# The first stage's instructions in another order, from a planner with other durations and priorities

## The reference, cut to what matters

```python
q, k, v = layernormed 4-to-1 channel mixes of layernorm(x)      # "read", three outputs of 256
o = causal softmax attention, 16 heads of 16, rope on q and k
h = h * A_full(o) + out(o) * B_full(o)                           # "write": softplus, exp, reciprocal
g, u = layernormed channel mixes of h
m = silu(g @ ctx...) * (u @ ctx...)                              # MLP to 1024
h = h * A_full(m) + out(m) * B_full(m)                           # second "write"
x = x + ...
W = mean_w + mean(|w - mean_w|) * sign(w - mean_w)               # for w1, w3, w2, 3584 x 1024 each
y = x + (silu(n @ W1.T) * (n @ W3.T)) @ W2.T                     # n = layernorm(x)
```

## Time and profile before

| | us |
|---|---|
| median of 3 runs | 1407.24 |
| lowest, highest | 1401.03, 1408.16 |
| the profiled execution, its own time | 1408.62 |
| its span in the trace | 1406.8 |
| mean granted TensorE clock over the span | 0.958 |

### The profile page before, as it was taken

One profiled execution on the slowest core, in us unless ns is written; L12 is line 12 of the kernel. 1 busy time (PEld: TensorE's weight loads), 2 busy tenths in 40 slices (PEclk: granted clock), 3 DMA queues, 4 the chain that ended last, 5 costly groups with the idle time before them and its releaser, 6 DMA issues.

```text
span 1406.8 us, 16747 instructions
## 1 busy us (share of the span) xinstructions
PE 1292.9 (92%) x6548; PEld 1015.8 (72%) x6548; DVE 868.6 (62%) x1135; ACT 530.1 (38%) x809; POOL 361.9 (26%) x197
## 2 busy tenths in 40 slices
PE   4887788877887899999999999999999999999998
PEld 4754555545665678888888888888788888888887
DVE  6768777778878865546564546363645546554544
ACT  4776665855655432222222222222222222222220
POOL 2222333233234422222222222222222222222210
PEclk9998988987899899999999999999999999999999
DMA  8476887577731222322222222232222232222312
GB/s 339 147 273 252 287 285 267 208 288 274 268 132 31 105 90 93 105 102 90 90 94 97 109 90 90 90 106 102 91 90 90 95 111 94 90 90 90 116 34 120
DMA packets 53826, 197.55 MB, mean 140 GB/s; under 512 B 6626, under 2 KB 6900, under 8 KB 53236
## 3 DMA queue, kind: packets, MB, share of 16 engines
q1 hardware_dynamic: 53748, 196.49, 38.7%
HBM read 192.27 MB, written 4.19 MB: 140 GB/s over the span
## 4 chain that ended last, share of the span: by engine, by line
PE 72%; DVE 15%; issue 5%; ACT 5%; DMA 2%; POOL 1%; SPq 0%; DVEq 0%; ACTq 0%
PE pair L969 42%; PE quad L1068 17%; PE pair L952 2%; DVE negwide L1372 2%; PE quad L915 1%; DMA ctxw<-in_mean_w 1%; DVE raw_w L1448 1%; DVE hid L1438 1%; PE pair L1022 1%; PE quad L905 1%; PE pair L843 1%; ACT prob L1122 1%; PE pair L824 1%; DVE wr_q L1425 1%; DVE big L1547 1%
## 5 line engine op out<-in xcount | busy, mean ns | idle before, releaser
L1633 POOL TENSOR_TENSOR raw_w<-raw_w,raw_base 128x1024 f32<-128x1024 f32 x84 | 215.5, 2567 | 661.5 <-DMA raw_base<-in_mean_w 661.5
L969 PE MATMUL pair<-xnT_hi,w_hi 128*128 128x512 f32 x880 | 343.8, 391 | 3.3 <-DVE xnT_lo L1557 3.3
L969 PE MATMUL pair<-xnT_lo,w_hi 128*128 128x512 f32 x880 | 343.6, 390 | 0.0
L969 PE MATMUL pair<-xnT_hi,w_lo 128*128 128x512 f32 x880 | 343.5, 390 | 0.0
L1590 DVE TENSOR_TENSOR hf<-sgf,pair 128x512 f32<-128x512 f32 x56 | 38.5, 688 | 282.1 <-PE pair L969 282.1
L1182 ACT ACTIVATE w_hi<-raw_w 128x1024 fp32r<-128x1024 f32 x84 | 88.8, 1058 | 324.0 <-DVE raw_w L1448 323.8
L969 PEld LDWEIGHTS pair<-xnT_hi,w_hi 128*128 128x128 f32 x880 | 166.1, 189 | 38.6 <-issue 2.7
L969 PEld LDWEIGHTS pair<-xnT_lo,w_hi 128*128 128x128 f32 x880 | 165.9, 189 | 34.5
L969 PEld LDWEIGHTS pair<-xnT_hi,w_lo 128*128 128x128 f32 x880 | 165.9, 189 | 34.4
L1068 PE MATMUL quad<-w_hi,h_hi 128*128 128x512 f32 x448 | 175.4, 391 | 9.3 <-DVE hid L1570 9.3
L1448 DVE SCALAR_TENSOR_TENSOR raw_w<-raw_w,coeff,raw_base 128x1024 f32<-128x1024 f32 x84 | 166.8, 1988 | 19.9 <-ACT raw_w L1165 19.9
(11 more groups left out here) (234 smaller groups left out, 1561.4 us busy)
## 6 DMA issues: line engine op xcount, KB each, us to landing
raw_w<-in_w SPq DMA_DIRECT2D x84, 512.0 KB, 3.8
raw_base<-in_mean_w SPq DMA_DIRECT2D x84, 512.0 KB, 4.6
part<-in_w SPq DMA_DIRECT2D x28, 512.0 KB, 4.1
part<-in_mean_w SPq DMA_DIRECT2D x28, 512.0 KB, 5.3
ctxw<-in_w SPq DMA_DIRECT2D x28, 512.0 KB, 4.8
ctxw<-in_mean_w SPq DMA_DIRECT2D x28, 512.0 KB, 6.3
big<-in_w SPq DMA_DIRECT2D x20, 512.0 KB, 3.8
big<-in_mean_w SPq DMA_DIRECT2D x20, 512.0 KB, 4.8
```

Of the source, the lines that this page charges most:

```text
L969: a = pe.matmul(banks[gate_bank(u, b)], ww[:, k, :], xx[:, k, :], start=k == 0 and n == 0, stop=k == KF - 1 and n == 2)
L1633: pool.tensor_tensor(w[:, :], w[:, :], base[:, :], ALU.subtract).then_inc(f_diff, 1)
```

## The change

Only the planner's inputs and its arithmetic are changed. The steps' durations on paper are set to other values; durations are multiplied by a factor per engine (`SLOW`, PE 1.107, DVE 1.061, ACT 1.009, POOL 0.981) in `engine_and_time` but not in `weight`; an engine is free for its next step a little before the step's result is done (`AHEAD_OF`, 0.04 to 0.16 us); a load takes the SP queue 0.8 us (`ISSUE`) and lands 1.6 us (`LANDING`) and its own duration later, but not before the load ahead of it has landed (`landed`); `HOP`, the time from one engine to another, is 0.05 in place of 0.12; and `FIRST`, `AHEAD`, `MEASURE_WEIGHT` and `PULL`, which set the priorities, all have other values. `OWN`, a lead for single steps, is empty. `LOADED`, `MEASURER`, `LATER`, the dependences and the program text of all engines are unchanged. What comes out is another order of the same steps on each engine, with the choices of banks that go with it.

```diff
@@ -112,38 +112,42 @@
 
 
 
-RAT = [("PE", 1.35), ("DVE", 0.3), ("PE", 0.25), ("ACT", 0.3), ("PE", 0.5), ("ACT", 1.7), ("DVE", 1.85, 0.2),
-       ("ACT", 0.87), ("DVE", 2.5, 0.25), ("POOL", 1.85), ("POOL", 0.75), ("DVE", 2.05, 2.05)]
+RAT = [("PE", 1.48), ("DVE", 0.27), ("PE", 0.27), ("ACT", 0.26), ("PE", 0.59), ("ACT", 1.48), ("DVE", 1.52, 0.2),
+       ("ACT", 0.83), ("DVE", 2.68, 0.25), ("POOL", 1.81), ("POOL", 0.72), ("DVE", 1.94, 1.94)]
 WORK = {
-    "front": [("DVE", 1.75), ("POOL", 0.6), ("DVE", 0.2, 0.15), ("ACT", 1.25), ("PE", 1.1), ("ACT", 1.05), ("PE", 1.95),
-              ("DVE", 1.95, 0.2), ("POOL", 0.9), ("DVE", 0.2, 0.15), ("ACT", 1.75), ("PE", 0.85), ("ACT", 2.8),
-              ("PE", 2.75), ("DVE", 2.95, 0.7), ("PE", 1.1), ("ACT", 1.22)],
-    "turnmax": [("PE", 0.35), ("DVE", 0.45)],
-    "out": [("ACT", 0.4)],
-    "row": [("PE", 0.6), ("DVE", 0.75), ("PE", 0.35), ("ACT", 0.4)],
-    "back": RAT + [("PE", 1.1), ("DVE", 1.25), ("PE", 1.95), ("DVE", 1.45, 0.2), ("POOL", 0.75), ("DVE", 0.2, 0.15),
-                   ("ACT", 1.15), ("PE", 0.6), ("ACT", 1.88)],
-    "mlp": [("PE", 1.85), ("ACT", 0.42), ("DVE", 0.45)],
-    "finish": [("PE", 5.25)] + RAT[1:8] + [("DVE", 3.5, 1.25)] + RAT[9:] + [("SP", 2.0), ("POOL", 0.75), ("DVE", 1.75), ("POOL", 0.6), ("DVE", 0.2, 0.15)],
-    "measure": [("SP", 3.5), ("POOL", 2.4), ("ACT", 1.17)],
-    "x": [("SP", 2.0)],
-    "ctx": [("SP", 7.0)],
-    "diag": [("DVE", 4.0, 4.0)],
-    "raw": [("SP", 2.0), ("POOL", 2.4), ("ACT", 1.06)],
-    "coef": [("DVE", 0.35), ("PE", 0.35), ("DVE", 0.2)],
-    "prep": [("DVE", 1.3, 1.3), ("ACT", 1.08), ("DVE", 1.25, 1.25)],
-    "norm": [("ACT", 1.25), ("PE", 1.1), ("ACT", 1.05), ("DVE", 1.25)],
-    "early": [("PE", 1.4)] * 4,
+    "front": [("DVE", 1.71), ("POOL", 0.55), ("DVE", 0.15, 0.15), ("ACT", 1.24), ("PE", 1.04), ("ACT", 1.02), ("PE", 1.92),
+              ("DVE", 1.64, 0.2), ("POOL", 0.86), ("DVE", 0.16, 0.16), ("ACT", 1.48), ("PE", 0.83), ("ACT", 2.19),
+              ("PE", 2.76), ("DVE", 2.4, 0.7), ("PE", 1.04), ("ACT", 1.08)],
+    "turnmax": [("PE", 0.39), ("DVE", 0.42)],
+    "out": [("ACT", 0.38)],
+    "row": [("PE", 0.61), ("DVE", 0.72), ("PE", 0.39), ("ACT", 0.38)],
+    "back": RAT + [("PE", 1.04), ("DVE", 1.21), ("PE", 1.91), ("DVE", 1.25, 0.2), ("POOL", 0.7), ("DVE", 0.16, 0.16),
+                   ("ACT", 1.02), ("PE", 0.61), ("ACT", 1.51)],
+    "mlp": [("PE", 1.89), ("ACT", 0.38), ("DVE", 0.42)],
+    "finish": [("PE", 5.32)] + RAT[1:8] + [("DVE", 3.55, 1.25)] + RAT[9:] + [("SP", 1.65), ("POOL", 0.73), ("DVE", 1.71),
+                                                                           ("POOL", 0.55), ("DVE", 0.16, 0.16)],
+    "measure": [("SP", 3.3), ("POOL", 2.35), ("ACT", 1.25)],
+    "x": [("SP", 1.65)],
+    "ctx": [("SP", 6.6)],
+    "diag": [("DVE", 3.84, 3.84)],
+    "raw": [("SP", 3.3), ("POOL", 2.35), ("ACT", 1.05)],
+    "coef": [("DVE", 0.2), ("PE", 0.3), ("DVE", 0.15)],
+    "prep": [("DVE", 1.28, 1.28), ("ACT", 1.05), ("DVE", 1.22, 1.22)],
+    "norm": [("ACT", 1.24), ("PE", 1.04), ("ACT", 1.01), ("DVE", 1.21)],
+    "early": [("PE", 1.53)] * 4,
 }
 
 MEASURER = ("DVE", "DVE", "POOL")
-DIFFERENCE = {"DVE": ("DVE", 1.25, 1.2), "POOL": ("POOL", 2.4)}
+DIFFERENCE = {"DVE": ("DVE", 1.22, 1.22), "POOL": ("POOL", 2.35)}
 
 
 LATER = (42, 72)
 
 GATING = 2 * JT
-LANDING, HOP, TABLE = 2.5, 0.12, 1.3
+
+ISSUE, LANDING, HOP, TABLE = 0.8, 1.6, 0.05, 1.3
+
+AHEAD_OF = {"PE": 0.16, "DVE": 0.08, "ACT": 0.09, "POOL": 0.04, "SP": 0.0}
 LOADED = {("front", 0, 0): 6.0, ("front", 1, 0): 8.0, ("front", 2, 0): 19.0, ("front", 3, 0): 21.0, ("front", 4, 0): 27.0,
           ("front", 5, 0): 29.0, ("diag", 0, 0): 14.0, ("front", 0, 13): 17.0, ("diag", 1, 0): 25.0}
 
@@ -176,7 +180,8 @@
 
     stage, t, part = key
     found = found_work(stage, t, part)
-    return found[0], found[1], found[2] if len(found) > 2 else found[1] if found[0] == "POOL" else 0.0
+    slow = SLOW.get(found[0], 1.0)
+    return found[0], slow * found[1], slow * (found[2] if len(found) > 2 else found[1] if found[0] == "POOL" else 0.0)
 
 
 def found_work(stage, t, part):
@@ -186,11 +191,11 @@
         kind = SEQ_UNITS[t][0]
         cols = sum(piece[2] for piece in pieces(t))
         if stage == "use":
-            return ("DVE", 0.2 + 4 * cols / 960) if kind == "S" else ("ACT", 0.15 + 4 * cols * 0.00085)
+            return ("DVE", 0.15 + 4 * cols / 960) if kind == "S" else ("ACT", 0.16 + cols / 300)
         if stage == "weigh":
-            return "PE", 0.1 + 0.53 * cols / 256
+            return "PE", 0.22 + cols / 600
         masked = len(pieces(t)) if kind == "S" else sum(piece[0] * P >= GROUPS[SEQ_UNITS[t][1]][1] * HQ for piece in pieces(t))
-        return "PE", 0.1 + 0.71 * cols / 256 + 0.36 * masked
+        return "PE", 0.07 + cols / 600 + 0.11 * len(pieces(t)) + 0.44 * masked
     return WORK[stage][part]
 
 
@@ -350,7 +355,7 @@
     per = {"front": 2, "back": 2, "finish": 2, "row": 2, "norm": 2, "mlp": MT, "coef": 1, "raw": EARLY, "prep": EARLY,
            "early": EARLY, "measure": UNITS, "ctx": 1, "diag": 1, "x": TILES}.get(stage, QUADS)
     ahead = AHEAD.get(stage, ())
-    return (FIRST[stage][t // per] if stage in FIRST else 0.0) + (ahead[part] if part < len(ahead) else 0.0)
+    return (FIRST[stage][t // per] if stage in FIRST else 0.0) + (ahead[part] if part < len(ahead) else 0.0) + OWN.get(key, 0.0)
 
 
 def phase_one_order():
@@ -377,12 +382,13 @@
             missing = [y for y in users[x] if y not in weight]
             todo += missing
             if not missing:
-                weight[x] = engine_and_time(x)[1] + HOP + max([weight[y] for y in users[x]], default=0.0)
+                weight[x] = found_work(*x)[1] + HOP + max([weight[y] for y in users[x]], default=0.0)
                 todo.pop()
     for n in range(UNITS):
         for part in range(3):
             weight["measure", n, part] = MEASURE_WEIGHT * (UNITS - n)
     free_at = {"PE": 0.0, "DVE": 0.0, "ACT": 0.0, "POOL": 0.0, "SP": 40.0}
+    landed = free_at["SP"]
     done, order, banks, had, turned_had = {}, [], {}, {}, {}
     owner = [None] * 8
     turned, table = None, "exp"
@@ -465,11 +471,13 @@
             for x in (1, 2) if sets[n] else ():
                 deps[stage, t, x] += [sets[n] + (10,), sets[n] + (11,)]
             sets[n] = (stage, t)
-        free_at[engine] = start + us
+        free_at[engine] = start + (ISSUE if engine == "SP" else us - AHEAD_OF[engine])
         if way:
             shared.append((start + us - way, start + us))
             shared = sorted(x for x in shared if x[1] > min(free_at["DVE"], free_at["POOL"]))
-        done[key] = start + us + (LANDING if engine == "SP" else 0.0)
+        done[key] = start + us
+        if engine == "SP":
+            done[key] = landed = max(start + LANDING, landed) + us
         ready.remove(key)
         for x in users[key]:
             left[x] -= 1
@@ -481,20 +489,23 @@
 
 
 
-MEASURE_WEIGHT, PULL = 4.89, 0.00247
-FIRST = {"back": (-2.3, -2.4, -2.9, -2.9), "coef": (-14.3, 2.9), "ctx": (14.3,), "diag": (28.9, 31.7),
-         "early": (-27.2,), "fill": (1.4, 1.7, -1.1, -0), "finish": (-0.7, 0.1, -1.9, -5.7),
-         "front": (-4.4, -4.2, -4.5, -5.5), "measure": (0.1,), "mlp": (-1.6, -3.6, -3.1, -6.7),
-         "norm": (7.5, 6.9, -1, 0), "out": (-3.8, -4.9, 3.9, -0.3), "prep": (-4.4,), "raw": (-4.8,),
-         "row": (-1.2, -3, -1.7, -1.5), "turnmax": (4.2, 1.4, 0.3, -1.1), "use": (-1.6, -1.3, 1.6, -1.6),
-         "weigh": (5.7, 1.8, 0.4, -0.2), "x": (7.7,)}
-AHEAD = {"back": (2.7, 8.3, 4.3, 3.5, 15.9, 3.2, 3.8, 3.3, 2, 1.7, 3.8, 2.8, 2.2, 2.6, 1.8, 2.8, 7.3, 3, 2.4, 3.9, 3.2),
-         "coef": (11.8, 5.8, 7.2), "ctx": (-15.4,), "diag": (-30.8,), "early": (11.3, 10.6, 12.5, 10.8), "fill": (0.1,),
-         "finish": (-1.1, 2.8, 6.1, 2.1, 6.9, 0.1, 0.9, -0.5, 0.2, 2.6, -3.4, 8.2, 5.4, -1.9, -0.5, -5.6, 0.6),
-         "front": (5.9, 4, 5.7, 4.5, 12.8, 5.4, 8.8, 5.9, 14, 7.4, 5.2, 5.2, 3.7, 17.5, 5.2, 4.7, 5.2),
-         "measure": (7, 0.1, -0), "mlp": (0.6, 3.4, 8), "norm": (-4.4, -14.5, 3.5, 8.2), "out": (4.2,),
-         "prep": (8.1, 4, 2), "raw": (6.4, -1.8, 3), "row": (6.7, 3.8, 2.4, 3.6), "turnmax": (0.4, 1.4), "use": (2.1,),
-         "weigh": (-0.5,), "x": (-7.9,)}
+
+MEASURE_WEIGHT, PULL = 5.027, 0.00365
+FIRST = {"back": (-7.5, -7.6, -8.3, -8.1), "coef": (-3.8, 6.1), "ctx": (5.4,), "diag": (28.1, 26.3), "early": (-1,),
+         "fill": (12.9, 1, -0.6, -1.2), "finish": (-0.4, -2.1, -4.3, -12.1), "front": (-3.8, -3.9, -3.9, -6),
+         "measure": (0.1,), "mlp": (1, 0.5, -3.9, -5.9), "norm": (2.6, -4.4, -5.2, -1.8), "out": (-5.7, -3, -7.6, 5.1),
+         "prep": (-0.2,), "raw": (-7.6,), "row": (-0.9, -1.1, 0, -0.7), "turnmax": (12.5, 11.3, 1.5, 1.2),
+         "use": (-1.6, -1.6, 4.6, -1.9), "weigh": (6, 1.8, 0.2, -0.2), "x": (5.2,)}
+AHEAD = {
```

(9 more changed lines are left out.)

## The result

| | before | after |
|---|---|---|
| median, us | 1404.58 (4 runs, 1401.03 to 1408.16) | 1421.3 (4 runs, 1419.72 to 1421.55) |
| ratio | | 1.0116, 95% interval 1.0093 to 1.0138 |
| profiled execution, its span, us | 1406.8 | 1417.9 |

The change makes the kernel 16.7 us slower. The forecast was 6.7 us faster (1400.5 us), with a range from 1388 to 1414. It started from the 1407.24 us of three runs; with a fourth run the kernel before stands at 1404.58, and at 1403.4 to 1404.6 in the runs beside the experiments. The two profiled spans differ by 11.1 us only: the one of before belongs to an execution at the slow end of its runs (1408.62), the one of after to the fastest (1419.72).

A forecast was written before the change was run, and what follows sets the result against it. The first stage was taken as bound by dependences, with TensorE and DVE near 80% busy, the second by TensorE. Gains of 4.7 us (early weight blocks) and 2.0 (durations) made 6.7, so 1400.5 us from 1407.24; range 1388 to 1414.

The forecast's parts named there:

- Function tables: ScalarE's table loads in the first stage: one pair more or fewer, 0 with 2.6 us either way.
- Front, attention, back: First-stage steps of these parts reshuffled by new leads: taken as 0, with 5 us either way.
- Durations on paper: Planner's MLP and second-write times on TensorE corrected, 11.3 us more work seen: 2.0 us of gain.
- The early weight blocks: POOL's three weight differences move later, out from under DVE's last finishing steps: 4.7 us of gain.
- rival B: First stage: nothing measurable, the differences only move to other DVE steps of the same chain; 1407 us, chance 0.23.
- The SP queue: Loads on SP reordered past measure, x and finish loads where the queue has slack: zero, covered by 23 us.
- The clock: TensorE's granted clock in the first stage: groups swap levels, 2.27 us per set of sixteen products, 0 net.
- C: Rival: TensorE's first gate product waits for a late weight block on DVE, 7.2 us slower; 1414.4 us, chance 0.17.
- A: Rival: first-stage holes on TensorE close and its clock stays up; 1395 us, chance 0.20.

The follow-up runs named there:

- new480_old: First 480 of the 1061 first-stage steps in the changed kernel's order, the rest in the order of the kernel before; 1427.6 us, 23.2 over before.
- old900_new: First 900 of the 1061 first-stage steps in the order of the kernel before, the rest in the changed order; 1406.91 us, 2.5 over before.
- search_5: Old order's steps moved one at a time to lower the changed planner's price under jittered durations, carried on from an earlier search; 1353.05 us, ratio 0.9634 to before.
- old720_new: First 720 of the 1061 first-stage steps in the order of the kernel before, the rest in the changed order; 1416.04 us, 11.4 over before.

## Why the prediction was wrong

Two terms that were put at nothing cost the time, and the two gains of which the sum is made did not reach the end of the stage.

**Function tables: "one pair more or one fewer; 0, with 2.6 us either way".** There were six pairs more. They cost 10.1 us, taken away from the new order, and 10.0 us, added to the old one. The reason given, that ScalarE has room, is an average: 303 of 492 us busy. The silu, DVE's product and the next silu go hand over hand through one buffer, so a load there can delay TensorE and DVE; which of the loads delay the end is not shown.

**Front, attention, back: "I take 0, with 5 us either way".** This bound is too small by far: the new front and first half of the attention, with the old order behind them, cost 23.2 us (new480_old), and the searched orders have the attention's end 33 to 40 us earlier than before. And the sum has no term at all for how `mlp` and `finish` are placed, while steps 720 to 900, where the third MLP half lies, make 9.0 us. Single leads (`front` part 6, `back` part 4) say little of either. The size was set by eye, with 72 and 82 us of idle time in view, and not from a row; the row that would have served for the placement is the half's 15.8 us, which doubled.

**Durations on paper: 2.0 us of gain.** That better durations make a better order was assumed. With the changed durations the old order's price is 468.6 us and the new one's 493.2: by its own paper the changed planner found a worse order than the one that ran. The sign of this term was wrong for the change as a whole. The change sets durations and priorities together, and no run has one without the other, so which of them spoils the order is open.

**The early weight blocks: -4.7 us.** The mechanism came true in place, but not as reasoned. The differences no longer lie in a row under the finishing steps; but they did not all move later, as their lower lead was taken to say. Before they began at 432.35 us; two of them now begin 17.0 and 13.6 us earlier, one 18.6 later:

```profile
415.40 2.35 POOL L1644 TENSOR_TENSOR raw_w<-raw_w,raw_base 128x1024 f32<-128x1024 f32 x1
...
418.74 2.35 POOL L1644 TENSOR_TENSOR raw_w<-raw_w,raw_base 128x1024 f32<-128x1024 f32 x1
...
450.95 2.34 POOL L1644 TENSOR_TENSOR raw_w<-raw_w,raw_base 128x1024 f32<-128x1024 f32 x1
```

DVE's L1449 (L1438 before) takes 0.94 to 1.40 us in all sixteen, where the two in the earlier trace rows took 1.88 and 2.76, and TensorE's wait ahead of the last pair's second write fell from 6.91 to 2.57 us. The forecast had named 2 us or less as its sign. The gain was local: everything arrived there 10.9 us late. And the contention of DVE and POOL moved with the order, as rival B had it: in the third half L1433 takes 2.01 us beside POOL's L1686 (401.73 to 404.12), where at 437.79, with POOL idle, it takes 0.18. The tail as a whole wins nothing (old900_new, +2.5).

**The SP queue, zero**: nothing in the runs speaks against it; SP still waits mostly for ScalarE, and the coefficients' first step comes 14.9 us earlier than before, at 414.09.

**The clock, 0 net.** The mean over the span is 0.958 in both profiled executions. But over 25 runs of before it is 0.962, over the four of after 0.958; among those 25 a clock higher by 0.010 goes with some 10 us less (1396.33 us at 0.969, 1409.56 at 0.960). By that, an estimate, 3 to 4 of the 16.7 us go with the clock; whether the waits bring the lower clock or it comes by itself these numbers don't tell. One piece has a price: TensorE's first products of the second batch begin at the lower level, thirteen of them 0.43 us apart where later ones are 0.23.

```profile
500.69 0.79 PE L980 MATMUL pair<-xnT_hi,w_hi 128*128 128x512 f32 x1 [2.37 <-DVE xnT_lo L1568]
501.28 0.63 PE L980 MATMUL pair<-xnT_hi,w_lo 128*128 128x512 f32 x1
```

That is 13 x 0.20 = 2.6 of the 3.1 us by which the second stage is longer; waits of 1.2, 1.1 and 2.4 us stand ahead of it. Before, after a wait of 0.98 us, the same products ran 0.23 us apart from the second on. The rule of the Trainium skill, TensorE: Matmul & The Clock Gate, section HAM oscillation, that what follows idle gaps runs cold, agrees with this place in direction. The prediction said that by it a looser order loses twice, but priced it as a rival on the fast side only.

**The rivals.** C had the sign, but its 1414.4 us are 6.9 below the measured time, and not by its mechanism: no wait of L980 for w_lo was found. A wait of its kind is there, 4.0 us of TensorE ahead of the first gate product of all, which the kernel before did not have at its 467.03:

```profile
473.70 0.77 PE L980 MATMUL pair<-xnT_hi,w_hi 128*128 128x512 f32 x1 [3.98 <-issue]
```

DVE's xnT_lo (L1568, 472.37 to 473.60) ends just before it, w_lo had been done since 469.07. B's time is out, and so is A's; A's mechanism, that the clock rises when holes close, fits search_5. The forecast named as its own refutation a second stage changed by over 2 us; that came, with 3.1.

**Slips in the numbers.** The 6.14 us in A are the mean of all eight sets of L952, not of five. The parts named for the lower end of the range, 6.9, 5 and 7.0, make 18.9 and not 19.2. Neither changes a reading.

## What to carry to other kernels

When a planner's durations are corrected, price the order that runs now with the new durations before anything else: here that one number, 468.6 against 493.2, had the sign, and a search from the old order by the same price won 51.6 us. Count what an order adds on its own account, such as function-table loads between silu and exponential, since "the same instructions" may not be the same. Where two engines pass one buffer back and forth, as silu and product do, look at the length of the whole series from first to last and at what is written into its gaps; busy shares don't show it. But test what such a length is worth at the end: here the third half doubled in one order, and was half as long again in one that is 51.6 us faster. A milestone such as the last attention copy tells more, and a glued order has to be looked at by it before it is taken as a test of anything.

## What was not expected of the hardware

24 table loads of 1.28 us cost 10.1 us by the medians in one order and 2.5 in another (the second within the noise), and twelve cost nothing that can be measured, or 10.0 where they came on top of twelve. TensorE's own busy time depends on the order: 391.8 us for 2589 products at a mean clock of 0.88, 365.6 for the same at 0.93. And fixed durations, summed along a fixed sequence, followed the chip over a range of 80 us: +24.6 on paper was +16.7 us, +10.7 was +2.5, +22.3 was +23.2, -51.4 was -51.6. The worst miss was 16.5 us (old720_new, +27.9 on paper and +11.4 measured), so such a price tells large differences apart and no small ones.
